# Attention scores of a small vision block: keys masked four ways in place, against keys spread by DMA

## The reference

```
b, s, d = x.shape              # 64 images, 25 tokens, 128 = 8 heads of 16
q1 = heads(x @ Q1_w.T)
k1 = heads(x @ K1_w.T + K1_b)
q2 = heads(x @ Q2_w.T)
k2 = heads(x @ K2_w.T + K2_b)
v = heads(x @ V_w.T)
a1 = softmax(einsum('bhqd,bhkd->bhqk', q1, k1) / scale)
a2 = softmax(einsum('bhqd,bhkd->bhqk', q2, k2) / scale)
lam = exp(lambda_q1 * lambda_k1) - exp(lambda_q2 * lambda_k2) + 0.2
attn = a1 - lam.reshape(1, H, 1, 1) * a2
o = einsum('bhqk,bhkd->bhqd', attn, v)
# then a norm over groups of 32 features x 25 tokens, the out projection, a residual and a layer norm
```

## Time and profile before

| | us |
|---|---|
| median of three runs | 237.5 |
| lowest and highest of them | 234.71 and 238.33 |
| profiled execution, its own time | 233.28 |
| span of the profiled execution | 231.5 |

### The profile page before, as it was taken

The page is one execution under the profiler, slowest core; times in us unless marked ns, Lnnn a source line. Parts: engine busy times, 40 slices in busy tenths (PEclk is TensorE's granted clock), DMA queues, the critical chain, the costliest instruction groups (busy, mean ns, idle before and its releaser), DMA issues.

```text
span 231.5 us, 8246 instructions
## 1 busy us (share of the span) xinstructions
PE 181.9 (79%) x3649; PEld 142.6 (62%) x3649; DVE 150.4 (65%) x335; ACT 102.6 (44%) x185; POOL 47.6 (21%) x64
## 2 busy tenths in 40 slices
PE   0799989999186595787899999999999999992000
PEld 0799975558144364675478888788887787871000
DVE  1333596567459999789965776666555454468960
ACT  2000047557213322413353667776775343325882
POOL 0000007302508668300000000000007000007660
PEclk9999999999859855558999999999999999998555
DMA  6999994253446400000000222131200000000012
GB/s 228 396 391 387 401 146 98 78 129 92 117 107 141 92 6 3 4 3 0 4 0 3 52 58 78 30 96 34 80 5 3 3 6 3 3 3 4 28 45 71
DMA packets 11108, 19.83 MB, mean 86 GB/s; under 512 B 2030, under 2 KB 6830, under 8 KB 10432
## 3 DMA queue, kind: packets, MB, share of 16 engines
q1 hardware_dynamic: 11072, 19.30, 28.5%
HBM read 15.20 MB, written 0.82 MB: 69 GB/s over the span
## 4 chain that ended last, share of the span: by engine, by line
PE 47%; DVE 31%; SPq 6%; issue 5%; ACT 4%; DMA 3%; POOL 2%; ACTq 0%; POOLq 0%
PE PS L1086 14%; PE PS L898 10%; DVE arena L302 7%; PE PS L1108 7%; PE PS L1098 4%; DVE t L649 3%; SPq L363 3%; DVE sm L703 2%; DVE mx L691 2%; ACT t L610 2%; SPq L350 2%; DVE st L851 2%; PE PS L1056 2%; PE PS L935 2%; DMA hid<-conv_filter 2%
## 5 line engine op out<-in xcount | busy, mean ns | idle before, releaser
L302 DVE COPY arena<-PS 128x1024 f32<-128x1024 f32 x32 | 39.0, 1224 | 32.4 <-PE PS L1086 32.4
L301 ACT ACTIVATE arena<-PS 128x1024 f32<-128x1024 f32 x32 | 32.7, 1025 | 22.4 <-PE PS L1086 22.3
L1086 PE MATMUL PS<-gates,wrow 18*128 18x128 f32 x1024 | 37.2, 282 | 1.7 <-DVE arena L302 0.7
L1086 PEld LDWEIGHTS PS<-gates,wrow 18*128 18x128 f32 x1024 | 31.4, 186 | 7.9 <-DVE arena L302 5.0
L898 PE MATMUL PS<-hid,arena 128*128 128x128 f32 (+1 forms) x208 | 26.7, 288 | 7.3 <-DVE hid L628 7.3
L898 PEld LDWEIGHTS PS<-hid,arena 128*128 128x128 f32 (+1 forms) x208 | 25.2, 198 | 8.7 <-issue 8.3
L957 PE MATMUL PS<-hid,arena 128*32 128x200 f32 x256 | 16.7, 421 | 10.0 <-DMA hid<-arena 10.0
L628 DVE TENSOR_REDUCE hid<-hid 128x256 f32<-128x1280 f32 x4 | 9.5, 2369 | 16.8 <-DMA hid<-conv_filter 16.8
L459 ACT ACTIVATE sd<-mv,epsc 128x2 f32<-128x2 f32 (+1 forms) x15 | 4.3, 292 | 35.7 <-DVE mv L639 35.7
L957 PEld LDWEIGHTS PS<-hid,arena 128*32 128x32 f32 x256 | 9.2, 132 | 16.3 <-DMA hid<-arena 11.8
L1108 PE MATMUL PS<-arena,t 128*32 128x128 f32 x512 | 17.3, 276 | 0.0
(11 more groups left out here) (106 smaller groups left out, 294.1 us busy)
## 6 DMA issues: line engine op xcount, KB each, us to landing
arena<-windows SPq DMA_DIRECT2D x24, 256.0 KB, 7.9
wrow<-ffn_weights SPq DMA_DIRECT2D x32, 128.0 KB
hid<-arena SPq DMA_DIRECT2D x32, 100.0 KB, 2.2
hid<-conv_filter SPq DMA_DIRECT2D x4, 640.0 KB, 7.3
cst<-consts SPq DMA_DIRECT2D x1, 1098.0 KB, 16.6
wrow<-ffn_weights SPq DMA_DIRECT2D x64, 8.0 KB
out<-t SPq DMA_DIRECT2D x16, 50.0 KB
arena<-windows SPq DMA_DIRECT2D x4, 64.0 KB, 8.1
```

The lines of the kernel that those rows point to most:

```text
L301: return eng.activation(dst, PS[:, b:b + 2, :], ACT.Copy)
L302: return eng.tensor_copy(dst, PS[:, b:b + 2, :])
L1086: mm = pe.matmul(PS[:, merge_bank(n) + r, :].rearrange("p (b k j) -> p k b j", k=4, j=NJ)[:, k], wrow[32 * r:32 * r + KR, w], gates[32 * r ...
```

## The change

The keys are no longer spread. A matmul of the scores now takes 64 partitions (half r, four heads) in place of 128, so that a key copy needs four masks, not eight: `headmask` has a column for each of the four heads in a half, and a key is copied four times. `kX` holds 4 x 1600 columns for each softmax, that of the first in `arena`, that of the second in `hid`. One image's scores are then two matmuls for each softmax, one a half, each with 4 heads x 25 = 100 columns moving: 32 matmuls a step, which write the halves to two banks. The DMAs of L363, the zeroing of `kE` (L405) and their semaphores go. GpSimd computes `headmask` from the constants ahead of the projections. The rest of the attention has its head order changed to fit, in tiles of the same sizes.

The order changes too. TensorE makes quarters 0 and 1, then scores 0 and 1, and the other two quarters between the next scores; v comes after scores 5. ScalarE takes the small exponential of lambda first, then copies q1 and k2 of quarters 0 and 1; both keys of quarters 2 and 3 come one after each of its first four exponentials, all four copies of v after the fifth, and the residual's bias (L529) after the sixth. VectorE copies k1 and q2 of quarters 0 and 1 and both queries of quarters 2 and 3, and no v.

The diff, without the semaphores, the lambda and probability layouts and the slices of `values`:

```diff
-        kX = take(2 * 2 * NTOK).rearrange("p (u b m k) -> p u b m k", u=NU8, b=2, m=2)
+        kX = [v.rearrange("p (u m k) -> p u m k", u=NU8, m=4) for v in (take(4 * NTOK), hid[:, 0:4 * NTOK])]
...
-        kE = hid[:, 0:2 * 2 * H * UI * NS].rearrange("p (s b h i k) -> p s b h i k", s=2, b=2, h=H, i=UI)
...
-            def spread_keys(u):
-                if u % 2 == 0:
-                    sp.wait_ge(proj_ready[1], 2 * (u // 2 + 1))
-                    sp.wait_ge(proj_ready[3], 2 * (u // 2 + 1))
-                if u < 2:
-                    sp.wait_ge(spread_zeroed, u + 1)
-                else:
-                    sp.wait_ge(scores_done, u - 1)
-                for r in range(4):
-                    f = slice(32 * r, 32 * r + 32)
-                    sp.dma_start(kEd[f, u % 2, :, r, :], kX[f, u].rearrange("p b m k -> p b (m k)")).then_inc(keys_spread[u % 2], 16)
-            for c in range(NC - 1):
+            for c in range(NC):
                 load_rows(0, c)
-            spread_keys(0)
-            spread_keys(1)
-            load_rows(0, NC - 1)
-            for u in range(2, NU8):
-                spread_keys(u)
...
+            groups = C("gnsum").rearrange("p (h a c) -> p a h c", h=2, a=2)[:, :, :, 0]
+            pool.tensor_tensor(rowhalf[:, :], groups[:, :, 0], groups[:, :, 1], ALU.add).then_inc(rowhalf_ready, 1)
+            pool.wait_ge(rowhalf_ready, 1)
+            pool.tensor_scalar(rowhalf[:, :], rowhalf[:, :], 32.0 * NS, None, ALU.mult).then_inc(rowhalf_ready, 1)
+            pool.wait_ge(rowhalf_ready, 2)
+            for i, name in enumerate(("even", "odd")):
+                pool.tensor_tensor(headmask[:, :].rearrange("p (a i) -> p i a", i=2)[:, i], rowhalf[:, :],
+                                   C(name).to_broadcast([P, 2]), ALU.mult).then_inc(headmask_ready, 1)
+            pool.wait_ge(headmask_ready, 2)
             for w, name in enumerate(("k1_b", "k2_b")):
-                for m, mask in enumerate(("even", "odd")):
-                    pool.tensor_tensor(kb[:, 2 * w + m:2 * w + m + 1], C(name), C(mask), ALU.mult).then_inc(kb_ready, 1)
+                pool.tensor_tensor(kb[:, 4 * w:4 * w + 4], headmask[:, :], C(name).to_broadcast([P, 4]), ALU.mult).then_inc(kb_ready, 1)
...
-            act.wait_ge(kb_ready, 4)
-            for c in range(NQ):
-                act.wait_ge(proj_done[0], c + 1)
-                act.activation(qT[0][:, c * QT:(c + 1) * QT], PS[:, 4, 0:QT], ACT.Copy).then_inc(proj_ready[0], 1)
-                act.wait_ge(proj_done[3], c + 1)
-                src = PS[:, 7, 0:QT].rearrange("p (u k) -> p u k", u=2)
-                for m, mask in enumerate(("even", "odd")):
-                    act.activation(kX[:, 2 * c:2 * c + 2, 1, m, :], src, ACT.Identity,
-                                   bias=kb[:, 2 + m:3 + m], scale=C(mask)).then_inc(proj_ready[3], 1)
             act.wait_ge(lprod_ready, 2)
             act.activation(lexp[:, :], lprod[:, :], ACT.Exp).then_inc(lexp_ready, 1)
+            act.wait_ge(kb_ready, 2)
+            def keys_evac(c, b):
+                w = 2 * b + 1
+                act.wait_ge(proj_done[w], c + 1)
+                src = PS[:, 4 + w, 0:QT].rearrange("p (u k) -> p u k", u=2)
+                for m in range(4):
+                    act.activation(kX[b][:, 2 * c:2 * c + 2, m, :], src, ACT.Identity,
+                                   bias=kb[:, 4 * b + m:4 * b + m + 1], scale=headmask[:, m:m + 1]).then_inc(proj_ready[w], 1)
...
+            for c in range(2):
+                act.wait_ge(proj_done[0], c + 1)
+                act.activation(qT[0][:, c * QT:(c + 1) * QT], PS[:, 4, 0:QT], ACT.Copy).then_inc(proj_ready[0], 1)
+                keys_evac(c, 1)
             for u in range(NU8):
                 act.wait_ge(shifted, u + 1)
                 act.activation(E[:, u % ES, :], E[:, u % ES, :], ACT.Exp, scale=HD ** -0.5).then_inc(exp_done, 1)
-                if u < 2:
-                    v_evac(2 * u)
-                if u == 2:
+                if u < 4:
+                    keys_evac(2 + u // 2, u % 2)
+                if u == 4:
+                    for v in range(4):
+                        v_evac(v)
+                if u == 5:
...
-            dve.wait_ge(kb_ready, 4)
-            for c in range(NQ):
-                dve.wait_ge(proj_done[1], c + 1)
-                src = PS[:, 5, 0:QT].rearrange("p (u k) -> p u k", u=2)
-                for m, mask in enumerate(("even", "odd")):
-                    dve.tensor_scalar(kX[:, 2 * c:2 * c + 2, 0, m, :], src, C(mask), kb[:, m:m + 1],
-                                      ALU.mult, ALU.add).then_inc(proj_ready[1], 1)
+            dve.wait_ge(kb_ready, 2)
+            def proj_evac(c):
+                if c < 2:
+                    dve.wait_ge(proj_done[1], c + 1)
+                    src = PS[:, 5, 0:QT].rearrange("p (u k) -> p u k", u=2)
+                    for m in range(4):
+                        dve.tensor_scalar(kX[0][:, 2 * c:2 * c + 2, m, :], src, headmask[:, m:m + 1], kb[:, m:m + 1],
+                                          ALU.mult, ALU.add).then_inc(proj_ready[1], 1)
+                else:
+                    dve.wait_ge(proj_done[0], c + 1)
+                    dve.tensor_copy(qT[0][:, c * QT:(c + 1) * QT], PS[:, 4, 0:QT]).then_inc(proj_ready[0], 1)
                 dve.wait_ge(proj_done[2], c + 1)
                 dve.tensor_copy(qT[1][:, c * QT:(c + 1) * QT], PS[:, 6, 0:QT]).then_inc(proj_ready[2], 1)
-            def v_evac(v):
-                dve.wait_ge(v_done, v + 1)
-                dve.tensor_copy(vtok[:, 4 * v:4 * v + 4, :], PS[:, 4 + v, :].rearrange("p (g c) -> p g c", g=4)).then_inc(v_ready[1], 1)
...
-            soft_shift(0)
+            proj_evac(0)
             dve.wait_ge(lexp_ready, 1)
             dve.tensor_tensor(neglam[:, 0:H], lexp[:, H:2 * H], lexp[:, 0:H], ALU.subtract).then_inc(neglam_ready, 1)
             dve.wait_ge(neglam_ready, 1)
             dve.tensor_scalar(neglam[:, H:2 * H], neglam[:, 0:H], -0.2, None, ALU.add).then_inc(neglam_ready, 1)
+            proj_evac(1)
+            soft_shift(0)
             soft_shift(1)
+            proj_evac(2)
             soft_sum(0)
-            v_evac(1)
-            v_evac(3)
             for u in range(2, NU8):
                 soft_shift(u)
+                if u == 2:
+                    proj_evac(3)
                 soft_sum(u - 1)
...
-            for c in range(NQ):
+            def proj(c, ws):
                 pe.wait_ge(h_ready, c + 1)
-                for w, name in enumerate(("q1", "k1", "q2", "k2")):
+                for w in ws:
                     if c >= 1:
-                        pe.wait_ge(proj_ready[w], (2 if w in (1, 3) else 1) * c)
-                    pe.matmul(PS[:, 4 + w, 0:QT], C(name), t2[:, c * QT:(c + 1) * QT], start=True, stop=True).then_inc(proj_done[w], 1)
+                        pe.wait_ge(proj_ready[w], (4 if w in (1, 3) else 1) * c)
+                    pe.matmul(PS[:, 4 + w, 0:QT], C(("q1", "k1", "q2", "k2")[w]), t2[:, c * QT:(c + 1) * QT], start=True, stop=True).then_inc(proj_done[w], 1)
...
-                pe.wait_ge(keys_spread[slot], 16 * 4 * (u // 2 + 1))
+                for w in range(4):
+                    pe.wait_ge(proj_ready[w], (4 if w in (1, 3) else 1) * (u // 2 + 1))
                 if u >= 2:
                     pe.wait_ge(shifted, u - 1)
-                for g in range(2):
+                for il in range(UI):
+                    im = u * UI + il
+                    i, nq = il % 4, NS if im % QI == QI - 1 else 32
                     for b in range(2):
-                        for i in range(4):
-                            im = u * UI + g * 4 + i
-                            mm = pe.matmul(PS[32 * i:32 * i + 32, 2 * slot + g, b * H * NS:(b + 1) * H * NS],
-                                           qT[b][:, im * NS:im * NS + 32], kE[:, slot, b, :, g * 4 + i, :], start=True, stop=True)
+                        c = (b * 2 + il // 4) * 4 * NS
+                        for r in range(2):
+                            f = slice(64 * r, 64 * r + 64)
+                            mm = pe.matmul(PS[32 * i:32 * i + nq, 2 * slot + r, c:c + 4 * NS], qT[b][f, im * NS:im * NS + nq],
+                                           kX[b][f, u, :, il % UI * NS:(il % UI + 1) * NS], start=True, stop=True)
                 mm.then_inc(scores_done, 1)
...
+            proj(0, range(4))
+            proj(1, range(4))
+            pe.wait_ge(h_ready, NQ)
             pe.wait_ge(pads_set, 5)
             scores(0)
             scores(1)
+            proj(2, range(4))
+            scores(2)
+            proj(3, range(3))
+            scores(3)
+            proj(3, [3])
+            scores(4)
+            scores(5)
             v_proj()
-            for u in range(2, 6):
-                scores(u)
-            pe.wait_ge(v_ready[0], 2)
-            pe.wait_ge(v_ready[1], 2)
+            pe.wait_ge(v_ready, 4)
             values(0)
...
```

38 lines of the change are left out of this document (18 added, 20 removed).

## The result

The changed kernel takes **224.98 us** (median of 4 runs, 224.75 to 228.59) beside 237.92 for the kernel before (4 runs on the same chip, 234.71 to 239.43): ratio 0.9526, 95% interval 0.9392 to 0.966 (the ratio leaves out the executions that stand more than 1.5% above the fastest of their own kernel; the two medians alone give 0.9456). It is faster, as forecast. The time stands 4.0 under the forecast 229.0, and 0.02 under the lower end of the range (225 to 236).

What follows compares the result with a forecast made beforehand. VectorE was taken to bound the attention up to the group sum; first maximum at 49.6 plus 33.4 of work and 0.5 of waits gives 83.5 against 92.02, gain 8.5; 237.5 - 8.5 = 229.0 us, range 225 to 236.

Steps and rivals of the forecast that it cites:

- What bounds the stage: First key copy to group sum, 49.0 us: VectorE bounds it, its 38.9 of work stays, 10.1 is idle.
- The new start: First softmax maximum, with scores begun after two projected quarters: starts at 49.6 us, not 53.88.
- The sum: VectorE from first maximum to group sum: 33.4 plus 0.5, group sum at 83.5 against 92.02, gain 8.5 us.
- the waits: VectorE between first maximum and group sum: 0.5 us added for waiting on other engines.
- The score step: TensorE's scores of one step in 64-partition tiles: 1.2 to 1.6 us, against 1.58 at full clock before.
- The tight place: v's projection and copies delay values 0 and scores 6, done at 71.9 to 72.3; VectorE wants them at 72.5 to 73.
- B: Clock falls in TensorE's pause before scores 5, v takes 7.8 us, scores 6 late: gain 6, time 231.5, chance 0.18.
- C: Clock stays full past the attention, chain after the group sum 1.5 us cheaper: gain 10, time 227.5, chance 0.12.
- D: 64-partition score tiles don't overlap, 2.7 us a step: gain 4 at full clock, time 235, chance 0.08.
- E: TensorE at half clock from near 48 becomes the bound, 2.9 us a score step: time 244, chance 0.05.
- F: ScalarE's key copies cost 0.75 not 0.6, four steps each 0.6 late: gain 4 or less, time 234, chance 0.10.
- the last addition: Whole time: the 8.5 us gain, made against the profiled 233.28, taken off the median 237.5, giving 229.0.

Runs made afterwards that it cites:

- b_no_spread: The kernel before with the spread DMAs taken out, its scores reading a zeroed tile: ratio 0.9642, first key copy to group sum 43.14 us.

## Why the prediction was right, and where it was off

**What bounds the stage: right.** VectorE's work stayed (38.9 to 38.40), its idle 10.1 became 1.19 and the third maximum's 5.76 went with the spread. b_no_spread gives 5.9 for the spread alone. What I read from the chain, spreads queued "behind each other and behind weight rows", was mostly the second: moving the weight rows gave 4.4.

**The new start: right.** 6.43 against 6.58. Undone, the order costs 6.04.

**The sum: right, a tenth too small.** 40.5 was forecast for the stage and 39.59 measured; the gain 8.5 should have been 9.4. The terms mis-sized are **the waits**, 0.5 forecast and 0.30 found, and **the softmax step**, priced at 3.22 and 3.18 here (65.06 to 68.24), times eight. The first maximum was 0.15 early, a pair of query copies 0.97 and not 1.05. The later start of 1.05 us, which no term covered, brought the whole difference back to 8.3. That the two profiled executions agree with 8.5 within 0.2 is therefore luck, and so is the group sum at 83.66 for a forecast 83.5.

**The score step: its bounds held, the value I took didn't.** I took 1.2 to 1.6, since "the rows of L957 are the nearest"; it was 1.10 to 1.19 at full clock and 1.88 at half. Nothing hung on it, but the "two to three microseconds to spare a step" were not there: TensorE had hardly a pause from 48.8 to 58.6, and scores 2 were done 1.5 us before VectorE asked for them (55.12 against 56.59). Three steps lie ahead of that point, so a step could have cost some 0.5 more, by an estimate from these rows. Its cause was only partly found: alternation of halves gives 0.2, what makes the rest of the fall from 1.58 was not separated.

**The tight place: right in place and order, with more room than forecast.** Scores 6 were forecast for 71.9 to 72.3 at full clock, and VectorE's wish for them for 72.5 to 73. They came at 72.64 at half clock with 0.8 to spare (VectorE asked at 73.43), and in the repeated run at 71.32 at full clock with 1.5 to spare (72.82).

**The rivals.** *B* named the right danger. The clock stayed full through the pause ahead of v (1.78 us; 1.0 to 1.8 in the seven executions above), and so v took 3.89, not 7.8; it fell at the next pause in three of them, where scores of 1.88 could still be in time. Why it stayed full at the first is open. *C* didn't come: the middle stretch is 32.06 for 31.96. Its condition, a clock that stays full past the attention, never came about (0.78 in that stretch, as before), so its price is untested. The two kernels that raised the mean clock there to 0.9 with idle matmuls took 34.0 and 33.9, and the group mean's delay (2.1 and 0.9) leaves nothing shorter than 31.9. *D* and *E* needed steps of 2.1 or more and found 1.1 to 1.9. The "gain 4" put to *E* at a step of 1.4 is 5.3 by the prediction's own sum, (1.4 - 1.0) x 8 = 3.2 less than 8.5. *F* needed 0.6 a step; 0.54 to 0.60 added to each of four steps cost nothing, so ScalarE's "just fits" was too tight. It set four copies and an exponential, 3.2, against a VectorE step of 3.22; but in three of these steps VectorE also has two query copies or a transpose, and they last 4.17, 4.11 and 4.36 (52.42 to 65.06).

**The time: the step that failed is the last addition.** "the forecast time is 237.5 - 8.5", as the prediction has it, sets a difference between two executions without the clock's fall under a median of executions most of which have it, and takes for granted that the changed kernel has it as often. That is why 224.98 came out just under a range whose lower end allowed for a gain of 12. Like against like the gain is 9.3 or 9.4: the medians of those without are 234.27 and 224.93, of those above 237 and near 228.6 they are 237.98 and 228.62. The other 3.6 of the 12.9 is how often the fall comes: 41 of 54 before, 4 of 10 in the changed kernel, 10 of 22 when its three variants with the same merges are counted in (bias later, halves apart, extra copies). That points to a share that the change moved, by what means no run tells; whoever reads only the medians credits the change with it. One thing in the traces goes with it and was not tested: of the seven profiled executions that have the changed attention and untouched merges, the three with the fall have their full clock from 11.17 to 11.36, the four without it from 11.68 to 13.09 (but the kernel with the scores late fell with 12.25, and of the kernel before's two executions the one with 10.65 fell and the one with 10.55 did not). That the fall itself makes the 4.5 is shown twice, in each kernel's repeated run. That a full matmul ahead of merges stops it rests on 6 of 6, which twelve of 22 without it would give by luck in (12/22)^6, 3 times in 100; it is a good sign and no proof.

## What to carry to other kernels

Before changing the arithmetic to be rid of a transfer, look at what stands ahead of that transfer in its queue: 24 issues of weight rows that nobody awaited yet were 4.4 of the 5.9 us here, and one moved line gave them back. List the idle time of the engine that bounds the stage by what ends it and cost each entry by itself: the larger part of this change, 6.0, was the softmax started behind half the projections, not the transfer. Forecast from one execution to the other, and ask apart from that what else the time of an execution hangs on, before the result is set under a median.

## What the runs showed of the hardware that I had not expected

- TensorE's clock at the first merges differs from execution to execution of the same code: in 120 to 122 us of the changed kernel it was 1.00 once (busy 1.74 of 2 us) and 0.65 the other time, after 1.74 of 2 us, and then 0.50 to near 130: 4.5 us. With one full 128 x 128 matmul ahead of the 16 thin ones (18 rows, 32 records) of four merges it stayed up in 6 of 6 executions, with two such merges in 5 of 6; luck is not ruled out.
- The place where the clock falls in the attention differs too, over the same code and pauses of much the same length: at 70.7 to 71.6 after 1.84 to 2.09 us without a matmul, or at 75.7 to 76.5 with 1.82 to 2.07 passed at full clock. One pause that "held" and one that "lost" are therefore no rule.
- How soon the clock is full at the start differs from 10.17 to 13.56 us, and the first key copy, 30 us later, moves with it by half as much (42.85 to 44.51).
- Idle matmuls ahead of short pauses saved nothing and cost 1.9 us in the middle stretch: TensorE was in time at half clock, and what was queued behind them was wanted.
- 32 matmuls of 64 rows and 100 columns take 1.10 to 1.19 us, 16 of 128 rows and 200 columns 1.58: the smaller tiles are quicker for the same columns in total, and halves in turn against halves one after the other make only 0.2 of it.
